# First feed-forward layer as seven block products, with the projection in f16 and every fourth low half on GpSimd

## What is computed

```
q = x @ Wq + bq;  k, v = ctx @ Wk + bk, ctx @ Wv + bv
attn = softmax(q k^T / sqrt(32), strictly causal); row 0 -> 0
x1 = layer_norm(x + (attn v) @ Wo + bo)
out = layer_norm(x1 + relu(x1 @ W1 + b1) @ W2 + b2)
```

## Time and profile before

| | |
|---|---|
| time, median of 3 runs | 2652.14 us (2651.48 to 2652.87) |
| profiled execution: time, span | 2651.14 us, 2649.3 us |
| mean granted TensorE clock | 0.989 of full speed |
| busy: TensorE, VectorE, ScalarE, GpSimd | 94%, 80%, 62%, 60% of the span |
| TensorE instructions | 22664 matmuls, as many weight loads |
| first layer (L1646) | 6144 matmuls, 756.2 us busy |
| second layer (L1662) | 5376 matmuls, 669.6 us busy |
| projection (L1632) | 768 matmuls, 193.5 us busy |
| VectorE low halves (L1599) | 256, 282.0 us busy |

### The profile page before, as it was taken

How to read it: one execution, slowest core, us unless ns; L and a number is a source line. 1 busy time by engine, 2 the same in 40 slices (tenths; PEclk the granted TensorE clock), 3 DMA queues, 4 the chain that set the end, 5 groups by cost and what they waited for, 6 DMA issues and landing times.

```text
span 2649.3 us, 62863 instructions
## 1 busy us (share of the span) xinstructions
PE 2498.2 (94%) x22664; PEld 1873.3 (71%) x22664; DVE 2116.9 (80%) x4886; ACT 1629.8 (62%) x2881; POOL 1585.5 (60%) x1721
## 2 busy tenths in 40 slices
PE   4899999999999999879999999999999999999998
PEld 1455555555555555557888888888888888888887
DVE  7999999999999999878767777767767676767675
ACT  2788889899899999886344444343444343444433
POOL 2677777777777777666455555555555555554543
PEclk9999999999999999989999999999999999999999
DMA  5344444443344443345232313222222222222220
GB/s 169 110 117 117 119 114 110 115 109 103 92 103 105 106 106 97 89 140 159 53 69 50 71 46 67 50 69 53 66 56 61 61 57 64 57 65 57 65 57 25
DMA packets 444456, 225.04 MB, mean 85 GB/s; under 512 B 302368, under 2 KB 388192, under 8 KB 444144
## 3 DMA queue, kind: packets, MB, share of 16 engines
q1 hardware_dynamic: 442544, 219.71, 32.5%
q10 hardware_dynamic: 1600, 1.31, 0.2%
HBM read 112.36 MB, written 57.69 MB: 64 GB/s over the span
## 4 chain that ended last, share of the span: by engine, by line
PE 63%; DVE 8%; SPq 8%; POOL 8%; issue 7%; DMA 4%; ACT 1%; ACTq 0%; DVEq 0%; POOLq 0%
PE h_ps L1646 23%; PE acc L1662 20%; POOL prob_lo L495 7%; PE front L1632 6%; PE lin_ps L934 5%; SPq L421 4%; PE max_ps L907 2%; PE st_ps L955 2%; DVE max_ps L886 2%; PE lin_ps L930 1%; PE o_ps L973 1%; SPq L458 1%; SPq L1065 1%; DMA heads<-stage 1%; PE st_ps L986 1%
## 5 line engine op out<-in xcount | busy, mean ns | idle before, releaser
L495 POOL TENSOR_TENSOR prob_lo<-probs,prob_hi 128x512 f16<-128x512 f32 (+1 forms) x768 | 797.8, 1047 | 335.2 <-ACT prob_hi L582 318.5
L1646 PE MATMUL h_ps<-x_halves,W 128*128 128x256 f16 x6144 | 756.2, 273 | 1.8 <-ACT hf L1431 1.7
L1662 PE MATMUL acc<-W,hs 128*128 128x256 f16 x5376 | 669.6, 273 | 0.3 <-DVE hs L1599 0.3
L1646 PEld LDWEIGHTS h_ps<-x_halves,W 128*128 128x128 f16 x6144 | 596.5, 98 | 87.5 <-issue 14.8
L1431 ACT ACTIVATE hf<-h_ps,b1s,scale_evac 128x256 f32<-128x256 f32 x512 | 284.9, 563 | 559.7 <-PE h_ps L1646 557.2
L1662 PEld LDWEIGHTS acc<-W,hs 128*128 128x128 f16 x5376 | 526.0, 98 | 61.4 <-DVE hs L1599 0.6
L1356 POOL TENSOR_TENSOR hf<-hf 128x256 f32<-128x256 f32 x256 | 243.4, 951 | 483.1 <-ACT hf L1431 482.7
L588 ACT ACTIVATE probs<-st_ps,exp_scale 128x512 f32<-128x512 f32 (+1 forms) x768 | 469.3, 611 | 98.2 <-PE st_ps L986 91.6
L886 DVE CUSTOM_DVE_ANT_0 max_ps<-max_ps,mask_q 128x256 f32<-128x256 f32 (+2 forms) x768 | 418.2, 560 | 47.1 <-PE max_ps L907 43.4
L582 ACT ACTIVATE prob_hi<-probs 128x512 f16<-128x512 f32 (+1 forms) x768 | 427.9, 557 | 23.0 <-issue 7.3
L1599 DVE TENSOR_TENSOR hs<-hf,hs 128x896 f16<-128x896 f32 x256 | 282.0, 1121 | 147.8 <-ACT hs L1420 147.7
(11 more groups left out here) (152 smaller groups left out, 3526.1 us busy)
## 6 DMA issues: line engine op xcount, KB each, us to landing
heads<-stage SPq DMA_DIRECT2D x748, 64.0 KB, 2.1
raw_c<-in_cT SPq DMA_DIRECT2D x64, 256.0 KB, 3.4
raw_x<-in_xT SPq DMA_DIRECT2D x64, 256.0 KB, 4.4
o_in<-ctx_rows SPq DMA_DIRECT2D x256, 64.0 KB, 2.5
x_in<-in_x SPq DMA_DIRECT2D x32, 512.0 KB, 4.0
x_rows<-x SPq DMA_DIRECT2D x64, 256.0 KB, 2.1
o_in<-x_rows SPq DMA_DIRECT2D x256, 64.0 KB, 2.4
out<-y SPq DMA_DIRECT2D x32, 512.0 KB, 3.0
```

What stands on the lines that cost most here:

```text
L495: pool.tensor_tensor(prob_lo[:, k % 4, 0:w], probs[:, k % PROBS, 0:w], prob_hi[:, k % 4, 0:w], ALU.subtract).then_inc(pl_done, 1)
L1646: last = pe.matmul(h_ps[:, f % 2, 0:T], W1[:, aw, j, f * P:(f + 1) * P], x1_halves[:, item.parity, aa, j, :], start=(j == 0 and m == 0), s ...
L1662: last = pe.matmul(acc_products[:, n, :], hs[:, p % HS, aa, n, :], W2[:, p, aw, n, :], start=(p == 0 and m == 0 and n % 2 == 0), stop=(p = ...
```

## The change

**First layer.** The 512 x 256 operand x1 and a 512 x 256 piece of W1 are seen as 2 x 2 blocks. Four mixes of each make seven products from which the four result blocks follow by additions (the Strassen-Winograd form). W1's mixes are made by GpSimd in attention windows 9 to 16 and stored to a new `mixed_w1`; x1's by GpSimd in each chunk (`X1_MIX`). A group `two` covers four blocks of 128 outputs. Its seven products of 2 x 2 x 3 matmuls of 128 tokens come in four steps (3, 1, 1, 2 products), and where two results share a term, PSUM goes on accumulating while ScalarE (`M2_AT`, `U2_AT`) and VectorE (`C11_AT`, `C22_AT`, `C21_AT`) take and complete partial results in between. 12 products x 16 = 192 matmuls of 256 columns a chunk become 84 x 4 = 336 of 128.

**Evacuation.** A pair's relu is now three ScalarE operations: one of 128 columns from PSUM (`C12_AT`), one of 128 and one of 256 from the SBUF tile `h_sums`.

**Projection.** Wo is scaled and split in f16; `front` is one bank, and the halves are in slots 4 and 6. Wo is loaded in attention window 1 and scanned there. The product of bv with Wo is four f32 matmuls in place of twelve.

**Low halves.** Of eight pairs, the fourth and the eighth get their low half from GpSimd.

**y.** x1 has one buffer; `y` shares memory with the weight ring and starts from x1 read back from HBM (`Y_LOAD`), to which GpSimd adds b2. Statistics of y come one slot after its sums instead of four (`STATS2`). `FFN2` is 12 slots behind `FFN1`; the feed-forward runs one more window. 56 weight pieces instead of 44.

```diff
-    OTR = 2
-    PROJ = 5
-    RES = 6
+    OTR = 2
+    ADD_BO = 3
+    PROJ = (4, 6)
+    RES = (5, 7)
     NORM1 = 8
     X1_TURN = 13
-    FFN1 = 16
-    FFN2 = FFN1 + 6
+    X1_MIX = (X1_TURN + 2, X1_TURN + 4)
+    X1_HI = (X1_TURN + 3, X1_TURN + 5)
+    X1_LO = (X1_TURN + 4, X1_TURN + 6)
+    FFN1 = 18
+    STAGES = (0, 2, 3, 5)
+    M2_AT = FFN1
+    C11_AT, U2_AT, C22_AT, C21_AT, C12_AT = FFN1 + 1, FFN1 + 2, FFN1 + 4, FFN1 + 6, FFN1 + 6
+    RELU = FFN1 + 7
+    MIX = FFN1 + 8
+    H_HI = FFN1 + 9
+    H_LO = FFN1 + 10
+    FFN2 = FFN1 + 12
     RES2 = FFN2 + FT
-    STATS2 = RES2 + 4
+    STATS2 = RES2 + 1
     NORM2 = RES2 + 8
...
+    STEPS = ((("b", 1, 1), ("a", 0, 0), ("d", 2, 2)), (("a", 5, 5),), (("a", 4, 4),), (("a", 6, 3), ("d", 3, 6)))
...
-        front = held.enter_context(nc.psum_tensor("front", [P, 2, 512], F32))
-        h_ps = held.enter_context(nc.psum_tensor("h_ps", [P, 2, 512], F32))
+        front = held.enter_context(nc.psum_tensor("front", [P, 512], F32))
+        mix_b = held.enter_context(nc.psum_tensor("mix_b", [P, 4, P], F32))
+        mix_ad = held.enter_context(nc.psum_tensor("mix_ad", [P, 2, 4, P], F32))
...
+        def first_product(item, two, stage):
+
+            if stage == 0:
+                wait_for(pe, x1_lo, 2, item, 1)
...
+                wait_for(pe, h_last, PAIRS, item, 2 * two + 2 - 4)
+                wait_for(pe, c21_done, TWOS, item, two + 1 - 2)
+                wait_for(pe, m2_kept, TWOS, item, two)
+            elif stage == 1:
+                wait_for(pe, x1_lo, 2, item, 2)
+                wait_for(pe, c11_done, TWOS, item, two + 1)
+            elif stage == 2:
+                wait_for(pe, u2_kept, TWOS, item, two + 1)
+            else:
+                wait_for(pe, c22_done, TWOS, item, two + 1)
+            for name, at_w, at_x in STEPS[stage]:
+                for r in range(2):
+                    for j in range(2):
+                        for m, (aw, aa) in enumerate(((0, 0), (0, 1), (1, 0))):
+                            opens = stage == 0 and name != "d" and r == 0 and j == 0 and m == 0
+                            last = pe.matmul(region(name, two)[:, r, :], w1_of(2 * two + r, aw, at_w)[:, j, :],
+                                             x1_halves[:, item.parity, aa, at_x, j, :], start=opens,
+                                             stop=(j == 1 and m == 2), skip_group_check=True)
...
                 for u in range(U):
-                    for item, _ in due(window, s, SLOTS, CHUNKS, PROJ + u):
-                        wait_for(pe, turned_lo, 2 * U, item, u + 1)
-                        wait_for(pe, res_done, U, item, u + 1 - U)
+                    for item, _ in when(window, s, PROJ[u]):
+                        wait_for(pe, ctx_lo, U, item, u + 1)
+                        wait_for(pe, res_done, U, item, u)
...
+                for item, k in when(window, s, H_LO, FT):
+                    if k % 8 == 6:
+                        p = k // 2
+                        wait_for(pool, h_hi, PAIRS, item, p + 1)
+                        pool.tensor_tensor(hs[p % HS][:, 1, :, :], hf[:, (PAIRS * item.n + p) % HF, 1:1 + PRODUCTS, :],
+                                           hs[p % HS][:, 0, :, :], ALU.subtract).then_inc(h_lo_fourth, 1)
```

More of the change, by code:

```diff
@@ L64, in __init__, with due @@
         self.n, self.parity = n, n % 2
-def due(window, slot, slots, items, first, span=1):
-    for back in range(BACK + 1):
+def due(window, slot, slots, items, first, span=1, behind=BACK):
+    for back in range(behind + 1):
         k = slot + slots * back - first
@@ L1016, in attention @@
     programs.o_read = (o_out, HEADS * B)
+    programs.scans_stored = (bounds.mix_stored, 48 * B)
+    programs.rows_stored = [(stored[i], 32 * GROUPS // 2 * B) for i in range(2)]
     return programs
@@ L1352, in gpsimd @@
+                for item, k in when(window, s, MIX, FT):
                     if k % 2 == 0:
@@ new lines, in scalar @@
+                for u in range(U):
+                    for item, _ in when(window, s, OTR + 1 + 2 * u):
+                        wait_for(act, ctx_turned, U, item, u + 1)
+                        if item.n == 0 and u == 0:
+                            act.wait_ge(*before.splits_done)
+                            act.wait_ge(*before.inputs_read)
+                        wait_for(act, proj_done, U, item, -U)
+                        act.activation(turned[:, item.parity, 0, :, u * P:(u + 1) * P], ctx_block(u), ACT.Copy
+                                       ).then_inc(ctx_hi, 1)
@@ new lines, in scalar @@
+                for item, k in when(window, s, M2_AT, FT):
+                    if k % 4 == 0:
+                        two = k // 4
+                        if item.n == 0 and two == 0:
+                            act.wait_ge(b1_scaled, 1)
+                            act.wait_ge(*before.heads_read[1])
+                        wait_for(act, m2_done, TWOS, item, two + 1)
+                        wait_for(act, h_out, FT, item, 4 * two - 4)
+                        act.activation(sums[:, two % 2, :, 2, :], region("b", two), ACT.Copy).then_inc(m2_kept, 1)
```

743 lines of the change are left out of this document (443 added, 300 removed).

## The result

The kernel became slower by 7%: 2844.74 us (median of 4 runs, 2842.41 to 2848.45) against 2652.51 us (4 runs, 2651.48 to 2654.56), a ratio of 1.0725 with a 95% interval of 1.0706 to 1.0744. The forecast was 2720 us with a range of 2640 to 2800. The direction was right, the size was not: 192 us more, where 68 were forecast.

A forecast was written before the change was run, and what follows sets the result against it. The prediction took TensorE to bound the feed-forward stage, at 44.85 us per chunk. Its sum was 2651.1 - 81 (work) + 122 (waits) + 15 + 2 (attention) + 10 (ramp) = 2719, given as 2720 us, range 2640 to 2800.

The forecast's parts named there:

- Part 1: TensorE's work per feed-forward chunk falls to 42.3 us, 2.5 less, in 32 chunks -81 us.
- Rival 3: Weight loads of 98 ns show behind 128-column first-layer matmuls: period 56.5 us, time 3049; chance 0.03.
- Chain A: From y's sums through VectorE and ScalarE to the next chunk's first first-layer group: TensorE stalls 2.4 us, 70 in all.
- Chain B: One-bank projection: second half waits for the first's residual, stall 1.5 us; first half about 0.2 late; 46 us in all.
- I follow the two longest chains: Part 2, waits: two chains in the new order give a period of 46.4 us, +122 us in all.
- The tail behind the last matmul keeps its operations: 0: End of the kernel, after the last matmul: same operations, so no added time.
- Ramp and attention: Ramp +10 us for more weight pieces and later second layer; attention +15 for W1 mixes and stores, +2 for Wo.
- rival 4: More GpSimd work slows chain A's two-input SBUF passes on VectorE by 2.65 us per chunk: 2797 us; chance 0.09.
- Rival 1: Feed-forward waits hide and TensorE stays the bound: 2597 us, faster; chance 0.13.

The follow-up runs named there:

- e9: e6 plus, in slot 0, ScalarE's x1 high half and four-block copy ahead of the evacuation, and x1's second transposition behind y's sums; 2663.6 us.
- run 336: Not a follow-up run: the words say that 336 first-layer matmuls of 128 columns go by in each chunk; no time of its own.
- e4: The changed kernel with ScalarE making the second turned context's high half one slot earlier; 2803.6 us.
- e3: The changed kernel with VectorE making the low half ahead of x1's roots and norm in slot 8; 2789.3 us.
- e15: The changed kernel with only y's two centring passes moved later, to RES2 + 7; 2803.8 us.
- e12: The kernel before the change, with y's statistics, variance and centring three slots earlier; 2707.1 us.
- e2: The changed kernel with y's statistics, variance and centring two slots later; 2824.2 us.
- e5: The changed kernel with the edits of e2, e3 and e4 together; 2752.5 us.
- e6: The changed kernel with the edits of e3 and e4, and only y's centring six slots later; 2683.2 us.
- e13: e9 with VectorE's low half also ahead of y's roots and norm in slot 6; 2665.2 us.
- e8: The changed kernel without GpSimd's four mixes of each W1 block in the attention stage; 2832.2 us.

## Why the prediction was wrong in size

**Part 1, TensorE's work: right.** 56 ns for a first-layer matmul, 2.59 us for half a projection, 42.3 us in all. e9 shows the prize to be real: 43.5 us per chunk when the waits are small. Rival 3, visible weight loads, fell. The 128-column matmuls run 336 to a chunk at 56 ns with a load of 98 ns each. The Trainium skill, "TensorE: Matmul & The Clock Gate", section "Back-to-back issue gap", has about 81 ns for such a stream; the trace disagrees, with groups of 36 in 2.01 us.

**Chain A: the size was right, in part by luck, and the catch one step off.** Forecast 2.4, measured 2.5 of idle time, 2.7 in the forecast's measure. The sentence that failed is "the third group of the chunk before, which waits for a copy behind the same x1 work on ScalarE, fits inside it". It did not fit inside: that group is where TensorE stood. Up to there the chain has ScalarE's copy (0.58) where the forecast had VectorE's low half of x1 (1.29), so it should have been 0.7 shorter; but statistics, variance and centring of y took 3.9 us (2064.70 to 2068.56) for a forecast of 3.06, and the low half ahead of them 1.4 (2062.94 to 2064.37) for 1.00. The errors nearly cancel.

**Chain B: right, a little smaller.** Forecast 1.5 and 0.2; measured 1.1 (1.3 in the forecast's measure) and nothing for the first half. e4 removed it.

**The step that failed: "I follow the two longest chains".** Three more costs stand in the mean steady period, and none is in the sum:
- The hf buffer, 1.3 us of idle time: an evacuation waits for the low half three pairs back, which stands behind x1's norm. e3 removes it and gains 55 us, more than any other single edit. The prediction followed what produces TensorE's inputs; it never asked what frees the buffers they pass through. e15 and e12 show the same link lengthened.
- The wait for y's sums, 0.6 us, which e9 cuts to under 0.2.
- The slow clock, 0.7 us. The prediction took a stall to cost its own length. In e2, e5 and e6, where the longest single wait is 1.7 us or less, the granted clock is 1.00; in e3 with a longest wait of 2.2 it is 0.98. The length alone does not decide it: the same stall of 2.5 us is followed by the 1.2 GHz level in every second chunk only, and one of 3.15 us in e12 is not followed by it at all. What decides stays open.

What the forecast did list, 46.4, came in its own measure to 42.3 + 2.7 + 1.3 = 46.3. The two waits in the same measure are 1.5 and 0.7, the clock is 0.7, and 0.3 are left (the first group behind the longest stall, and what I can't place): together the 3.2 up to 49.5. The period lies 3.1 above the forecast, and over 31 periods that is the steady error of 95 us; the two waits make 68 of them.

**The end: wrong.** "The tail behind the last matmul keeps its operations: 0" is true of the operations (2831 to the end, 12 us, as before), and misses what lies between the last projection and there. The second layer starts 12 slots behind the first instead of 6, and the first layer 2 slots later. The deeper pipeline was put into the ramp alone, as idle time. In e9, whose end takes 21.0 us more than before, the rows behind the last projection split it: 612 first-layer and 420 second-layer matmuls for 312 and 336 before, 9 us more at full pace; 9.0 us idle, 6.84 of them in one wait for a low half, where before there is none; and the rest mostly a granted clock of 0.77 in the last 9 us of matmuls. The changed kernel has these too, and three of its four steady stalls (1.29, 0.57 and 2.49 us) once more. e13 takes 2 us away.

**Ramp and attention: about right.** +9.7 for +10, though this figure leans on the long steady period that it is set against: in e9, where the period is short, the same first chunks make it +22.9. And +13.1, about 10 in the mean of the kernels, for +17. e8 gives nearly all of it to GpSimd's mixes, as the forecast had it from the windows with and without W2's mixes.

**GpSimd and VectorE hindering each other (rival 4): small.** The low half's mean is 1.18 us in the steady stretch (128.8 / 109) for a shortest row of 1.08, and at 2062.94 it takes 1.51 while GpSimd mixes (its passes run from 2061.97 to 2068.09 without a gap). The Trainium skill, "GPSIMD Engine Reference", section "Key points", says that the two share SBUF interfaces; the trace agrees, but the sizes are small: beside that 0.1 us, a centring pass of y has a mean of 0.97 us where one of x has 0.74. The rival needed 2.65 us per chunk on chain A; the low half and two centrings make 0.6.

**Rival 1, that the waits hide,** was given 0.13. It needed another order, and even with that (e9) the steady stretch gives 1.4 of the 2.5 us per chunk that it says. Those 43 us are less than what the attention stage (9), the ramp (23) and the end (21) take, so that even this order does not beat the kernel before.
